# A small audio tower on one Trainium2 core: the opening of the attention chunks rebuilt without selection products

## The reference

```python
# token part
x_diff = concat([0, x[t] - x[t-1]])                    # over time
x_emb  = x_diff @ W_ve.T + b_ve                        # 32 -> 128
x_lr, x_rl = ewma(x_emb), reversed ewma(x_emb)         # alpha 0.1, forward and backward
h = 0.5 * (x_lr + x_rl) @ W_lin.T + b_lin
# attention on layernorm(h)
v_w, o_w = basis @ v_coeffs.T, basis @ o_coeffs.T
q, k = l2norm(x @ shared_q_w), l2norm(x @ shared_k_w)  # norm over all 128 columns
v = x @ v_w                                            # then 4 heads of 32 columns
scores = (q k^T) * decay_h ** (j - i - 1) for j > i, else 0
h += (scores @ v) @ o_w.T * out_scale
# feed-forward on layernorm(h)
h += gelu(x @ tril(W1).T + b1) @ tril(W2).T + b2
```

## Time and profile before

| | us |
|---|---|
| median of 3 runs | 84.05 |
| the runs | 84.0, 84.05, 87.06 |
| the profiled execution | 83.98 |
| its span in the profile | 82.3 |

### The profile page before, as it was taken

How to read it: one execution, slowest core, us unless ns; L and a number is a source line. 1 busy time by engine, 2 the same in 40 slices (tenths; PEclk the granted TensorE clock), 3 DMA queues, 4 the chain that set the end, 5 groups by cost and what they waited for, 6 DMA issues and landing times.

```text
span 82.3 us, 2682 instructions
## 1 busy us (share of the span) xinstructions
PE 68.0 (83%) x1047; PEld 51.4 (63%) x1047; DVE 60.6 (74%) x177; ACT 40.9 (50%) x94; POOL 37.4 (45%) x48
## 2 busy tenths in 40 slices
PE   2996759964975899855999999999999997978840
PEld 2984648641143784645967996798679975845730
DVE  5799999999056493994998599848993599694250
ACT  1536345679365200494765366626663624574420
POOL 5935194396563700278423833292409100667800
PEclk9999999999999999999999999999999999999997
DMA  0960000001433100000000040003000300003043
GB/s 8 288 228 0 0 0 0 8 0 52 104 97 93 39 0 0 8 0 0 0 8 4 0 132 1 0 8 125 4 0 8 115 14 8 0 0 125 0 137 113
DMA packets 3826, 3.55 MB, mean 43 GB/s; under 512 B 2171, under 2 KB 3189, under 8 KB 3814
## 3 DMA queue, kind: packets, MB, share of 16 engines
q1 hardware_dynamic: 3474, 3.06, 12.9%
q10 hardware_dynamic: 340, 0.32, 1.2%
HBM read 1.08 MB, written 1.54 MB: 32 GB/s over the span
## 4 chain that ended last, share of the span: by engine, by line
PE 61%; DVE 20%; ACT 7%; issue 7%; POOL 1%; DVEq 0%; ACTq 0%; POOLq 0%
PE s_ps L971 8%; PE s_ps L1059 6%; PE a_ps L1026 6%; PE r_ps L1000 6%; PE s_ps L1076 5%; PE r_ps L986 5%; PE s_ps L875 4%; PE k_ps L929 3%; DVE prob L658 3%; PE s_ps L917 3%; DVE ident_and_centring L551 2%; PE r_ps L1047 2%; PE a_ps L951 2%; DVE ss_row L633 2%; ACT L501 2%
## 5 line engine op out<-in xcount | busy, mean ns | idle before, releaser
L658 DVE TENSOR_TENSOR prob<-s_ps,dmask 125x500 f32<-125x500 f32 x24 | 15.0, 673 | 1.7 <-PE s_ps L971 1.5
L340 POOL TENSOR_TENSOR h_b<-h,w_ffn 125x512 f32<-125x512 f32 (+1 forms) x7 | 7.8, 1133 | 11.4 <-DVE h L722 9.2
L318 POOL TENSOR_TENSOR q_dec<-qT,powers 128x500 f32<-128x500 f32 x5 | 5.8, 1163 | 9.8 <-ACT qT L403 9.8
L433 ACT ACTIVATE xn<-h,rstd 125x128 f32<-125x128 f32 x20 | 6.4, 390 | 5.8 <-POOL rstd L330 5.8
L301 POOL TENSOR_TENSOR quad<-gram_z,z 128x250 f32<-128x250 f32 (+1 forms) x6 | 5.9, 997 | 5.0 <-ACT gram_z L467 3.7
L722 DVE SCALAR_TENSOR_TENSOR h<-a_ps,rec,h_tok 125x128 f32<-125x128 f32 x22 | 6.2, 343 | 2.2 <-PE a_ps L1026 2.2
L971 PE MATMUL s_ps<-qT,kT 32*125 32x125 f32 x192 | 6.9, 279 | 0.9 <-ACT gram_z L467 0.9
L708 DVE TENSOR_TENSOR y<-s_ps,h_b 125x512 f32<-125x512 f32 (+1 forms) x6 | 3.9, 647 | 4.8 <-PE s_ps L1076 4.8
L971 PEld LDWEIGHTS s_ps<-qT,kT 32*125 32x125 f32 x192 | 5.9, 183 | 2.4 <-issue 2.1
L1026 PE MATMUL a_ps<-o_T,rT 128*125 128x128 f32 x44 | 5.9, 274 | 1.9 <-ACT h_tok L416 1.9
L330 POOL TENSOR_TENSOR rstd<-ve,minus_half 125x4 f32<-125x4 f32 (+1 forms) x7 | 6.6, 944 | 0.6
(11 more groups left out here) (175 smaller groups left out, 147.2 us busy)
## 6 DMA issues: line engine op xcount, KB each, us to landing
out_dram<-y SPq DMA_DIRECT2D x5, 224.0 KB
z_stk<-z_hi SPq DMA_DIRECT2D x8, 62.5 KB, 2.1
z_stk<-z_lo SPq DMA_DIRECT2D x4, 62.5 KB, 2.1
out_dram<-y SPq DMA_DIRECT2D x2, 112.0 KB
w_base<-in_w_base_dram SPq DMA_DIRECT2D x1, 192.0 KB, 3.6
w_ffn<-in_w_ffn_dram SPq DMA_DIRECT2D x1, 192.0 KB, 3.6
xt<-in_x_dram SPq DMA_DIRECT2D x1, 188.0 KB, 3.0
w_tok<-in_w_tok_dram ACTq DMA_DIRECT2D x1, 162.0 KB, 3.2
```

What stands on the lines that cost most here:

```text
L340: pool.tensor_tensor(h2_b[n][:, b0:b1, :], h2[n][:, b0:b1, :], b2_row.unsqueeze(1).broadcast_to([C, b1 - b0, D]), ALU.add)\
L433: act.activation(xn[n][:, b, :], h2[n][:, b, :], ACT.Copy, scale=rstd2[n][:, b:b + 1])\
L658: dve.tensor_tensor(prob[i % 2][:, h, :, :], sc_ps[h][0:C, 0:W4].rearrange("p (b t) -> p b t", b=B), dmask[:, h, :].unsqueeze(1).broadcast ...
```

## The change

- **Queries and keys of chunks 0 and 1** no longer come from the stack. ScalarE writes high words of `z` for that chunk into `z_hi` (now 752 columns wide), VectorE low words into `z_lo`, and `early_qk(j)` multiplies each batch's own 32 rows with the weights' words: 2 x 3 x 4 = 24 fp32r products of 32 rows, 128 weight columns and 126 moving columns, four row groups into four PSUM banks. The bias is added on eviction (`early_queries`, `early_keys`). The weights' words `w_hi`, `w_lo` come from a centred `wqk_c` and `proj` repeated for four batches.
- **No selections**: `pick`, `select`, `select_high`, `select_low` go. The stacks of chunks 0 and 1 are made by 12 further transfers on SP, ahead of the 12 that were there.
- `w_stk` is filled by three products into one bank (`stacks`), one eviction and one subtraction.
- **ScalarE's opening** is reordered; `w_tok` (now 164 columns instead of 324) and `w_att` are fetched earlier. The sums of the norms are evicted by ScalarE (`sums_out`), the maximum moves behind the turn (`squared`, VectorE).
- **VectorE**: the centring moves up, the decay's small operations ahead of the forward scans, the four dmask scans ahead of the four probs of chunk 0.
- **GpSimd**: its large memset of `z_stk` now also waits for the centring; `xd` no longer waits for `z1_ok`; `part_z` now waits for the last backward scan; `gram_z` has three buffers instead of two; `distance(1)` comes before the last quads.
- **TensorE**: `scores(0)` and `scores(1)` stand ahead of the sums and the large forms; four warm-up products instead of six.

Cut to the core ("..." marks what is left out):

```diff
-            for part, src in ((0, z_hi), (2, z_hi), (1, z_lo)):
...
+            sp.wait_ge(hi0_ok, 1)
+            sp.wait_ge(hi1_ok, 1)
+            stack(0, z_hi, NC - 2, NC, zstk0_d)
+            stack(2, z_hi, NC - 2, NC, zstk0_d)
+            sp.wait_ge(lo0_ok, 1)
+            sp.wait_ge(lo1_ok, 1)
+            stack(1, z_lo, NC - 2, NC, zstk0_d)
+            sp.wait_ge(zhi_ok, 1)
+            stack(0, z_hi, 0, NC - 2, zstk_d)
+            stack(2, z_hi, 0, NC - 2, zstk_d)
+            sp.wait_ge(zlo_ok, 1)
+            stack(1, z_lo, 0, NC - 2, zstk_d)
...
             pool.wait_ge(x10_ok, 1)
-            pool.wait_ge(z1_ok, 1)
             pool.wait_ge(tril_ok, 2)
...
             pool.wait_ge(fwd_ok, 2)
+            pool.wait_ge(bwd_ok, 3)
             pool.wait_ge(rest_ok, 1)
...
+            TERMS = ((w_hi, z_hi), (w_hi, z_lo), (w_lo, z_hi))
+            def early_qk(j, banks):
...
+                for n, (col, landed) in enumerate(((Q0, q_s), (K0, k_s))):
+                    for term, (weights, words) in enumerate(TERMS):
+                        for b in range(B):
+                            rows, at = slice(b * CH, (b + 1) * CH), b * 512 + n * (C + 1)
+                            ins = pe.matmul(banks[:, at:at + C + 1], weights[rows, col:col + D],
+                                            words[rows, (LAST - j) * C:(NC - j) * C + 1],
+                                            start=(term == 0), stop=(term == len(TERMS) - 1))
+                    ins.then_inc(landed, 1)
...
+            early_qk(0, s_ps)
+            early_qk(1, kra_ps)
+            scores(0)
             forms()
+            stacks()
             for piece in range(3):
                 quads(piece)
+            scores(1)
...
+            sums(0)
+            quads(3)
+            turn_sums(0)
+            quads(4)
             project_kv(0)
             project_h(0)
             retrieve(0)
             carry(0)
+            quads(5)
             project_kv(1)
             attention_out(0)
```

More of the change, by code:

```diff
@@ L273, in _ @@
             pool.wait_ge(half_ok, 1)
+            pool.wait_ge(centre_ok, 1)
+            for words in (z_hi, z_lo):
+                pool.memset(words[:, T:T + 2].bitcast(F32), 0.0).then_inc(pad_ok, 1)
+            pool.wait_ge(pad_ok, 2)
             pool.memset(z_stk[3 * CH:STK, :, :, :].bitcast(F32), ONE).then_inc(zone_ok, 1)
@@ L299, in quads @@
                 pool.wait_ge(gz_ok, piece + 1)
-                pool.wait_ge(z1_ok, 1)
-                pool.tensor_tensor(quad[:, a, t0:t1], gram_z[piece % 2][:, 0:t1 - t0], z[:, t0:t1], ALU.mult)\
+                if group == 0:
+                    pool.wait_ge(z0_ok, 1)
+                    pool.wait_ge(z1_ok, 1)
+                pool.tensor_tensor(quad[:, a, t0:t1], gram_z[piece % 3][:, 0:t1 - t0], z[:, t0:t1], ALU.mult)\
                     .then_inc(late_ok, 1)
@@ L306, in _ @@
             pool.wait_ge(zhi_ok, 1)
-            pool.tensor_tensor(z_lo[:, :], z[:, rest], z_hi[:, :].bitcast(F32), ALU.subtract).then_inc(zlo_ok, 1)
-            for piece in range(3, 6):
-                quads(piece)
+            pool.tensor_tensor(z_lo[:, rest], z[:, rest], z_hi[:, rest].bitcast(F32), ALU.subtract).then_inc(zlo_ok, 1)
             def distance(i):
@@ L342, in add_b2 @@
                     .then_inc(h2b_ok, 1)
+            for piece in range(3, 5):
+                quads(piece)
             distance(1)
+            quads(5)
             for i in range(1, LAST):
@@ L383, in _ @@
[L383 to L396 removed]
+            act.activation(proj_T[:, 0, :], a_ps[:, 2 * D:2 * D + STK], ACT.Copy).then_inc(projc_ok, 1)
@@ new lines, in _, with high_words @@
+            act.wait_ge(qkrep_ps, 1)
+            act.activation(w_hi[:, :], k0_ps[:, 0:2 * D], ACT.Copy).then_inc(whi_ok, 1)
+            act.wait_ge(qkbias_ps, 1)
+            act.activation(qk_bias[:, :], r_ps[:, 2 * D:2 * D + 2], ACT.Copy, scale=ONE).then_inc(qkbias_ok, 1)
+            def high_words(j):
+                span = slice((LAST - j) * C, (NC - j) * C)
+                act.wait_ge((z0_ok, z1_ok)[j], 1)
+                act.activation(z_hi[:, span], z[:, span], ACT.Copy).then_inc((hi0_ok, hi1_ok)[j], 1)
@@ L765, in _ @@
             keys(0)
-            probs(1, 0)
+            probs(1, 2)
             carry_on(0)
-            for h in range(1, H):
-                probs(1, h)
+            probs(1, 3)
             values(1)
-            sums(1)
+            keys(1)
             residual(0)
-            keys(1)
             statistics(0)
+            squared(1)
             scales(1)
@@ L1115, in _ @@
             sums(1)
-            project_qk(2)
-            turn_sums(1)
             retrieve(1)
             project_h(1)
+            project_qk(2)
             carry(1)
+            turn_sums(1)
             attention_out(1)
```

417 lines of the change are left out of this document (204 added, 213 removed).

## The result

| | before | after |
|---|---|---|
| median of the runs | 84.03 | 85.47 |
| the runs | 84.05, 87.06, 84.0, 83.99 | 85.95, 85.09, 85.1, 85.83 |
| the profiled execution | 83.98 | 85.95 |
| its span | 82.3 | 83.9 |
| its mean granted clock | 0.993 | 0.977 |

The changed kernel is slower: ratio 1.018, 95% interval 1.009 to 1.026. The ratio lies within two per cent, the interval reaches beyond. The time is outside the range of the prediction (80.3 to 85.0), and above the time before, where a gain, to 83.0, was forecast.

The account below looks back on a forecast made before the run. TensorE's full stretch from 38.9 to 65.8 us was taken as the bound, so only its earlier start counts. ffn_turn(0) would end at 39.7 against 40.63: 83.98 - 0.95 = 83.0, range 80.3 to 85.0.

Parts of the forecast that it names:

- Part 1: VectorE's opening to the end of the 500-column scan: it ends at 12.65 against 13.41, gain 0.75.
- Part 2: From the 500-column scan to scores(1): dmask to 16.05, probs to 18.5, scores(1) at 18.6 instead of 26.02.
- Part 3: From scores(1) to scores(2): 10.4 and 5.85 of work, waits 0.65 and 1.7; scores(2) at 37.2, 1.7 earlier.
- both collisions: VectorE's nrm and sc_v each meet a running GpSimd quads on the SBUF port; retrieve(0) waits 1.7.
- Transfers: Twelve more issues on SP at 0.65 each, landed by 21.05, needed at 24.2: they cost nothing.
- Part 4: From scores(2) to ffn_turn(0), which waits for xn(0): ends at 39.7 against 40.63, 0.95 gained; TensorE full as before afterwards.
- Were POOL not there, 14.05: End of VectorE's four dmask scans without GpSimd's alternating part_z and z; 16.05 with them.
- The 16.6 for PE: When TensorE finishes scores(0), forms, stacks and three 250-column forms ahead of scores(1), 1.9 before probs are ready.
- Escape from the port: Rival: sc_v comes before GpSimd's quads(4), 1.1 earlier, 81.9; if nrm escapes too, 81.4; chance 0.20.
- DVE first: Rival: VectorE keeps the port through four dmask scans, done at 14.05; 2.1 earlier, 80.9; chance 0.20.
- Products don't overlap: Rival: early_qk's new products don't overlap, or ScalarE bounds; sums_out(0) 0.7 late, 83.7; chance 0.12.
- The port holds more: Rival: GpSimd's memset also holds VectorE's scans, 1.0, and holds last whole instructions, 0.8; 84.8; chance 0.14.

Follow-up runs that it names:

- the filled run: Changed kernel with four more unread products, two behind the projection and two behind the bias products: 85.08 (81.22 to 87.32).
- the last experiment: Changed kernel with eight warm-up products and GpSimd's quads(3) held until the scales of group 0 are made: 80.31, ratio 0.953.
- filling the wait: Changed kernel with quads(5) ahead of retrieve(0) on TensorE and gram_out(5) ahead of r_out(0) on ScalarE: 83.83.
- scales first: Changed kernel with GpSimd's quads(3) and quads(4) held until the first group's scales are done: 82.28; with six warm-up products 80.48, with eight 80.31.
- dmask first: Changed kernel with six warm-up products, quads(5) ahead of retrieve(0), GpSimd's quads(3) behind the scales, and part_z behind four dmask scans: 83.33, ratio 0.974.
- the fillers: Changed kernel with six warm-up products, quads(5) ahead of retrieve(0), GpSimd's quads(3) behind the scales, and six more unread products: 81.43, ratio 0.948.

## Why the prediction was wrong, point by point

**Right, by the rows.** Part 1: centring 0.16, first forward scan at 5.17 (forecast 5.35), the 500-column scan alone in 1.25, ending at 12.73 (12.65). Part 2 on DVE: last dmask at 16.04 (16.05), probs at 18.36 (18.5). Part 3: both collisions, and 1.87 of PE's idle time before retrieve(0) where 1.7 was forecast. Transfers: TensorE waited for none of the stack's twelve new ones, though their issues took 0.72 each instead of 0.65 for the first eight.

```profile
z_stk<-z_hi SPq DMA_DIRECT2D x8, 31.2 KB, 2.0
```

They cost nothing, as said. Part 4's rule, that from ffn_turn(0) on nothing changes, held to a tenth: it ends at 40.63 before and 42.24 after (41.12 + 1.12), 1.6 later, and the span is 1.6 longer.

**Small misses.** (They add up: in the filled run with 81.22 us, all of it at the full level from 7 us on, ffn_turn(0) ends at 37.81, 1.9 before the forecast. So with TensorE at its full level, as the prediction assumed, the time would still have missed 83.0, on the low side, though within the range.) xd did not get in ahead of z: z took 0.37 and z0 was there at 7.73, not 8.85. That gain reached nobody, since ScalarE's high words of chunk 1 stood behind the evictions that waited for PE's slow opening: DVE was idle for 1.68 before its last z_lo, and the big scan started at 11.48 anyway. The right end came by the wrong road, and by luck: with the fast opening of the filled run the big scan starts at 10.52 and scores(1) at 17.56, 1.0 before the forecast. "Were POOL not there, 14.05" is 0.2 too late by its own terms (12.65 and four scans of 0.3). The 16.6 for PE fits its terms only if scores(0) end at 13.7, not start there; at full level PE was ready at 16.1 (14.64 + 1.47).

In Part 3 the wait of 0.65 for the key powers did not come, since the powers scan ran at 19.38, ahead of POOL's z_lo; in its place PE waited 0.85 for POOL's quads ahead of sums(0). Also the walk from retrieve(0) to scores(2) was 0.7 too long at the full level: 10.3 forecast, 9.6 in the runs at full clock (25.16 to 34.77). In Part 4 POOL's chain behind q_dec was 0.5 too short:

```profile
38.05 1.16 POOL L344 TENSOR_TENSOR q_dec<-qT,powers 128x500 f32<-128x500 f32 x1 [1.69 <-ACT qT L443]
...
39.49 1.04 POOL L356 TENSOR_TENSOR rstd<-ve,minus_half 125x4 f32<-125x4 f32 x1
```

It runs q_dec, ve and rstd one after another, behind PE's queries of chunk 2, so xn on ScalarE follows the start of scores(2) by 1.4 and ffn_turn(0) ends 3.05 behind their start, in the changed kernel and in the last experiment alike, not 2.5.

**The step that failed.** Part 2's "the stacks 0.9, three forms of 250 columns at 0.5 each: 16.6. So PE is ready 1.9 before probs are", and with it every duration of Part 3. All were taken from rows at TensorE's full level, and I never asked at which level the changed opening would run, though the diff takes two of six warm-up products away and the earlier trace rows begin at 12.83, past the slow part. In the opening PE then needs 2.06 for scores(0) instead of 1.15, 1.95 for the stacks (15.97 to 17.92) instead of 1.0, 1.83 for the three forms of 250 columns against 1.47; early_qk, forecast at 0.9 for 24 products, takes 1.4 there (first group 10.40, seventh 11.78), and 0.7 at the full level. PE is ready at 19.68 instead of 16.6, and takes the bound from DVE: scores(1) come 1.1 behind the forecast, and 2.1 behind the 17.56 of the fast opening. Then the 1.7 us wait, which I priced as a wait and nothing more, was followed by three microseconds at the lower level: quads(5) 1.89 for 1.04, keys and values 1.15 for 0.74, carry 0.68 for 0.48: 1.5 more.

The account closes. Against the forecast, scores(1) are 1.1 late (opening), the walk to retrieve(0) 0.1 long, the walk to scores(2) 0.8 long (the fall's 1.5 less the 0.7 above), and ffn_turn(0) another 0.55: 2.54 in all, 42.24 against 39.7. With the 0.37 more that lie outside the span (85.95 - 83.9 = 2.05, against 1.68) this makes 83.0 + 2.54 + 0.37 = 85.9, the profiled 85.95. The 0.37 outside the span is not explained. The runs support the two large terms apart from each other: with the opening left slow, filling the wait gave 1.6 in the medians and removing it 3.2 (the wait and the fall). The 2.9 of six warm-up products hold both terms, since its profiled execution has no fall behind the wait either: of the 3.6 us by which its scores(2) are earlier, 1.6 are there at scores(1), 1.5 come behind retrieve(0).

**The rivals.** "Escape from the port" and "DVE first" did not happen; both mechanisms are real, as the runs with scales first (nrm 0.17) and dmask first (1.32) show, but they need an added wait. "Products don't overlap" is false: at the full level four of them take 0.11, less than the 0.14 of one product of L951 (at the lower level they take 0.21 to 0.27). "The port holds more" gave the nearest time by luck and was wrong in its mechanism: the last dmask ended at 16.04, not 16.85, and the scan and the product at 3.09 and 3.78, beside the memset, took 0.48 and 0.29, so a memset does not hold a DVE instruction with two SBUF inputs. On the memset the Trainium skill (SBUF — State Buffer, "SBUF: two separate sides") had it right in its second half. One thing beside the memset was held, L624's TENSOR_SCALAR of four columns, 0.79, as the prediction said of its kind.

**What stays open.** Which condition raises the level in the opening. Rows: with eight warm-up products it rose by 7 us in one profiled execution and not before 20 in another; with six, near 5 to 6 in two, near 20 in two others, at 13.8 in a fifth, with the fillers. More warm-up came with more short executions, which I take for fast openings (of the changed kernel 0 of 10 executions came in under 84, with eight products 4 of 6; with scales first, one in four came in under 80.6 with four products, and all six with eight), it doesn't ensure it. And a wait of 1.87 to 1.89 was followed by a fall in the profiled executions with a slow opening (the changed kernel twice, eight products) and by none in those with six products alone and with filler alone. Nor is it the length of one wait that decides: 0.91 was followed by no fall where quads(5) stand first, 0.89 by one in the kernel before with four warm-up products, and with six products and the scales first the level fell at 12.7 with no wait over 0.40 near it.

## What to carry to other kernels

Before taking a TensorE duration from a trace, look at which level it ran, and ask whether the change alters what the engine does before that point: warm-up products, fillers and waits can change the price of everything behind them. The wait of 1.9 us cost nearly its length twice here, once as a wait and once as slow work behind it (1.5); one wait added on another engine, so that a short VectorE instruction meets no running GpSimd one, removed both. And run a kernel whose level is not settled many times, the kernel before included: four executions of one program spread over 6 us here.

## What the runs showed of the hardware that I had not expected

- The granted clock column reads 1.00 in the opening while a 128-column fp32 pass is recorded with 0.42 us and scores take 2.06; later in the same execution they take 0.28 and 1.15.
- The same instructions have fast and slow openings: two programs that are alike up to GpSimd's quads(3), with eight warm-up products, started scores(0) at 12.39 (1.15 long) and at 15.13 (2.06). One program's executions spread from 81.22 to 87.32 us.
- VectorE with two SBUF inputs is not held by GpSimd's memset (0.48 for 126 columns of scan), and is by its two-input operations (nrm 1.20 against 0.17).
- Four fp32r products of 32 rows in four row groups, 126 columns each: 0.11 us from one such four to the next at the full level, 0.21 to 0.27 at the lower.
- Four dmask scans and two GpSimd operations alternate: 3.39 for what takes 1.32 alone, and GpSimd's 1.24 and 1.27 don't stretch (the same 1.24 and 1.27 with dmask first).
